# One run of 64x64 products in a fused attention and convolution step

## The reference

```python
q = einsum('bhwd,de->bhwe', x, Q_P)
k = einsum('bhwkd,de->bhwke', stk, K_P)      # stk: the 9 shifted views of x, zero-padded
v = einsum('bhwkd,de->bhwke', stk, V_P)
scores = einsum('bhwke,bhwe->bhwk', k, q) * mask
alpha = softmax(scores)
t = x + einsum('bhwk,bhwke->bhwe', alpha, v)
t_in = t
t = relu(conv(t, ff1_kernel) + ff1_bias)
t = relu(conv(t, ff2_kernel) + ff2_bias)
t = relu(conv(t, ff3_kernel) + ff3_bias)
return t_in + t
```

## Time and profile before

| | |
|---|---|
| median of 3 runs | 2117.69 us (2116.01 to 2118.15) |
| profiled execution | 2115.95 us, span 2114.2 us |
| TensorE busy | 2053.2 us, 97% |
| VectorE busy | 1856.8 us, 88% |
| ScalarE busy | 1068.6 us, 51% |
| weight loads busy | 1229.9 us, 58% |
| granted TensorE clock, mean | 0.992 |
| mean HBM and on-chip traffic of the DMAs | 152 GB/s |

### The profile page before, as it was taken

How to read it: one execution, slowest core, us unless ns; L and a number is a source line. 1 busy time by engine, 2 the same in 40 slices (tenths; PEclk the granted TensorE clock), 3 DMA queues, 4 the chain that set the end, 5 groups by cost and what they waited for, 6 DMA issues and landing times.

```text
span 2114.2 us, 61688 instructions
## 1 busy us (share of the span) xinstructions
PE 2053.2 (97%) x23866; PEld 1229.9 (58%) x23866; DVE 1856.8 (88%) x2756; ACT 1068.6 (51%) x3021; POOL 17.2 (1%) x28
## 2 busy tenths in 40 slices
PE   4899999999999999999999999999999999999997
PEld 3565555655565655655656655655656665665544
DVE  4698899899899899899889899899889899889885
ACT  3555555455455455455455455455455455455421
POOL 3000000000000000000000000000000000000000
PEclk9899999999999999999999999999999999999998
DMA  5555454454454454454455454454455454455432
GB/s 144 132 160 148 157 167 143 153 171 141 151 171 144 151 174 141 151 173 144 150 168 145 151 170 147 151 167 149 150 172 142 151 172 147 149 168 155 138 126 85
DMA packets 286054, 320.89 MB, mean 152 GB/s; under 512 B 87802, under 2 KB 220218, under 8 KB 279482
## 3 DMA queue, kind: packets, MB, share of 16 engines
q1 hardware_dynamic: 285982, 319.92, 50.0%
HBM read 150.23 MB, written 33.82 MB: 87 GB/s over the span
## 4 chain that ended last, share of the span: by engine, by line
PE 91%; DVE 5%; ACT 1%; issue 1%; DMA 1%; SPq 0%; DVEq 0%; ACTq 0%
PE conv_banks L496 31%; PE conv_banks L458 15%; PE conv_banks L521 13%; PE side_banks L521 13%; PE side_banks L439 5%; PE side_banks L418 4%; PE conv_banks L398 3%; PE side_banks L427 3%; PE side_banks L449 3%; PE side_banks L410 1%; DVE work L945 1%; ACT relued L766 1%; ACT prob L708 1%; DVE tf L852 0%; DVE negmax L831 0%
## 5 line engine op out<-in xcount | busy, mean ns | idle before, releaser
L496 PE MATMUL conv_banks<-dodd,w3f 128*64 128x512 f32 (+2 forms) x1616 | 492.9, 582 | 11.2 <-DVE work L912 9.5
L496 PE MATMUL conv_banks<-deven,w3f 128*64 128x512 f32 (+2 forms) x1616 | 496.7, 585 | 2.2 <-DVE prob L841 2.2
L708 ACT ACTIVATE prob<-side_banks,negmax 128x100 f32<-128x100 f32 x1024 | 341.7, 363 | 293.1 <-DVE negmax L831 293.1
L458 PE MATMUL conv_banks<-dt,w1f 128*64 128x256 f32 (+2 forms) x4128 | 395.5, 381 | 2.7 <-ACT rq L720 2.6
L458 PEld LDWEIGHTS conv_banks<-dt,w1f 128*64 128x64 f32 (+1 forms) x4128 | 224.3, 135 | 186.7 <-issue 99.5
L496 PEld LDWEIGHTS conv_banks<-dodd,w3f 128*64 128x64 f32 x1616 | 149.3, 138 | 246.3 <-issue 222.2
L945 DVE TENSOR_TENSOR work<-side_banks,work 128x1024 f32<-128x1024 f32 (+1 forms) x130 | 153.3, 1226 | 110.6 <-PE side_banks L521 110.6
L496 PEld LDWEIGHTS conv_banks<-deven,w3f 128*64 128x64 f32 x1616 | 147.8, 137 | 153.9 <-issue 114.2
L708 ACT ACTIVATION_READ_ACCUMULATOR prob<-side_banks,negmax 128x1 f32 x1024 | 230.3, 225 | 0.0
L720 ACT COPY rq<-conv_banks 128x512 f32<-128x512 f32 x128 | 74.0, 582 | 305.7 <-PE conv_banks L398 305.7
L725 ACT COPY probt<-side_banks 100x1024 f32<-100x1024 f32 x128 | 124.2, 1020 | 177.9 <-PE side_banks L427 177.9
(11 more groups left out here) (92 smaller groups left out, 3184.6 us busy)
## 6 DMA issues: line engine op xcount, KB each, us to landing
xk<-x_keys SPq DMA_DIRECT2D x65, 800.0 KB
xc<-x_bands SPq DMA_DIRECT2D x65, 650.0 KB, 4.9
xr<-x_bands SPq DMA_DIRECT2D x260, 128.0 KB, 2.9
dodd<-dodd SPq DMA_DIRECT2D x65, 512.0 KB, 3.0
out<-work SPq DMA_DIRECT2D x64, 512.0 KB, 2.7
xs<-x_bands SPq DMA_DIRECT2D x130, 128.0 KB, 3.1
dt<-dt SPq DMA_DIRECT2D x65, 256.0 KB, 4.9
deven<-deven SPq DMA_DIRECT2D x65, 256.0 KB, 3.1
```

The lines of the kernel that those rows point to most:

```text
L458: mm = nc.tensor.matmul(bank[(LOWER, UPPER)[o], n * 256 + lo * 64:n * 256 + hi * 64], w1f[i][rows, m, s, o * C:o * C + C], dt[rows, lo + s ...
L496: mm = nc.tensor.matmul(bank[rows, lo_ * 128:hi_ * 128], w3f[:, m, s, odd * C:odd * C + C], source[:, lo_ + s // 2:hi_ + s // 2, m], start ...
L708: last = nc.scalar.activation(prob[:, g, a], score_banks[g // 2][:, g % 2, a * KEYS:(a + 1) * KEYS], ACT.Exp, bias=negmax[:, g, a:a + 1], ...
```

## The change

The 64x64 products of an ordinary step stand in one run: v_product, masks and scores of half 0, outer quarters, masks and scores of half 1, and only then all the wholes. For this the halves of side_banks swap their roles (half 0 of the scores, mix and its turned weights in the far banks, half 1 and the value product in the near ones; streams 2 and 3 of ODD in the near banks, those of EVEN in the far ones), and waits are placed anew: v_product waits for outer ODD, masks of half 0 for outer EVEN. Wholes go image by image, and middle1 and keep_u2 are cut in two, one for each image. The turn of half 1 goes from ahead of conv2 into the second go_on2, with a wait of its own. On VectorE add_x goes ahead of the input transforms of ODD, and outer3 goes ahead of scalings 2 and 3 and the second u_low. On ScalarE both copies of r go ahead of the ReLUs.

```diff
-        score_banks = (near_banks, far_banks)
+        score_banks = (far_banks, near_banks)
...
-                for n, m in enumerate((0, 3) if outer else (2, 1)):
-                    for i in range(2):
+                for i in range(2):
+                    for n, m in enumerate((0, 3) if outer else (2, 1)):
...
-            def go_on2(G, k, j):
+            def go_on2(G, k, j, ahead=None):
 
                 pe.wait_ge(du_low, G * 2 + (j // 2 + 1))
                 for s in range(2):
+                    if ahead and s == 1:
+                        ahead()
...
-            def await_turn(b):
-                pe.wait_ge(y_ready, b * 2 + 4)
-                pe.wait_ge(prob_ready, b * GROUPS + 3 * GROUPS)
+            def await_turn(b, half):
+                if half == 0:
+                    pe.wait_ge(y_ready, b * 2 + 4)
+                pe.wait_ge(prob_ready, b * GROUPS + (2 * GROUPS + 2 + 2 * half))
...
                     quarters(k, False, True)
-                    wholes(k, False, False, lambda: await_v(G, b, att))
                     if att:
+                        pe.wait_ge(dve_read, outer_read(G, ODD, 1))
+                        pe.wait_ge(y_ready, b * 2 + 2)
+                        pe.sem_inc(phase_begun)
                         v_product(b)
+                    if att == ASK:
+                        pe.wait_ge(dve_read, outer_read(G, EVEN, 1))
+                        pe.wait_ge(r_ready, b * 2 + 5)
+                        pe.sem_inc(phase_begun)
+                        masks(0)
+                        scores(b + 2, 0)
+                        pe.wait_ge(r_ready, b * 2 + 6)
+                        pe.sem_inc(phase_begun)
                     quarters(k, True, True)
                     if att == ASK:
-                        masks(0)
-                        scores(b + 2, 0)
                         pe.wait_ge(t_ready, b * 2 + 2)
                         pe.sem_inc(phase_begun)
                         masks(1)
                         scores(b + 2, 1)
+                    wholes(k, False, False)
                     wholes(k, True, False)
...
-                conv3_tile(G, k, 3, (lambda: await_turn(b)) if att == ASK else None)
+                conv3_tile(G, k, 3, (lambda: await_turn(b, 0)) if att == ASK else None)
                 if att == ASK:
                     turn(b + 2, 0)
-                    turn(b + 2, 1)
                 begin2(G, k, 0, b, att)
                 go_on2(G, k, 0)
                 begin2(G, k, 1, b, att)
-                go_on2(G, k, 1)
+                go_on2(G, k, 1, (lambda: await_turn(b, 1)) if att == ASK else None)
+                if att == ASK:
+                    turn(b + 2, 1)
...
                 if att == ASK:
                     keep_r(b + 2, 0)
+                    keep_r(b + 2, 1)
                 if p is not None:
                     relu_conv2(G, None, ODD, 1)
-                if att == ASK:
-                    keep_r(b + 2, 1)
-                if p is not None:
                     relu_conv2(G, None, EVEN, 1)
-                keep_u2(G, k)
+                keep_u2(G, k, 0)
+                keep_u2(G, k, 1)
...
                     outer(G, None, ODD, 1)
                     outer(G, None, EVEN, 1)
-                    inputs(G, None, ODD, 0, 1)
-                    inputs(G, None, ODD, 1, 1)
                 if att:
                     add_x(k, b, par, 1)
                     add_x(k, b, par, 0)
                 if p is not None:
+                    inputs(G, None, ODD, 0, 1)
+                    inputs(G, None, ODD, 1, 1)
                     inputs(G, None, EVEN, 0, 1)
-                middle1(G, k)
+                middle1(G, k, 0)
+                middle1(G, k, 1)
...
                 u_low(G, k, 0)
+                outer3(G, k)
                 if att == ASK:
                     scale(b + 2, 2)
                     scale(b + 2, 3)
                 u_low(G, k, 1)
-                outer3(G, k)
                 finish(G, k, b)
```

More of the change, by code:

```diff
@@ L44 @@
 FILLS = 12
[L45 removed]
+ACT_READS, DVE_READS, RELUS = 5, 9, 3
 def fill_of(which, j):
@@ L148, in build @@
         r_banks = conv_banks[:, 2:4]
-        score_banks = (near_banks, far_banks)
+        score_banks = (far_banks, near_banks)
         def conv2_bank(which, j):
-            return (conv_banks if j < 2 else side_banks)[:, bank_of(which, j % 2)]
+            return conv_banks[:, bank_of(which, j)] if j < 2 else side_banks[:, 2 * (which == EVEN) + j % 2]
         const_in = sem("const_in")
@@ L223, in filled, with act_reads, middle_read, half1_done @@
             return G * FILLS + (fill_of(which, j) + 1)
[L225 to L230, removed]
+        def act_reads(G, which, behind=0, image=1):
+            n = {CONV1: 1 + image, CONV3: 3, ODD: 4, EVEN: 5}[which]
+            return G * ACT_READS + (n + ACT_READS - ACT_READS * behind - (2 if G is FINAL else 0))
+        def middle_read(G, which, behind=0, image=1):
+            n = {CONV1: 1 + image, CONV3: 4, ODD: 6, EVEN: 7}[which]
+            return G * DVE_READS + (n + DVE_READS - DVE_READS * behind - (3 if G is FINAL else 0))
         def outer_read(G, which, behind=0):
-            n = {CONV1: 2, CONV3: 4, ODD: 7, EVEN: 8}[which]
-            return G * DVE_READS + (n + DVE_READS - DVE_READS * behind - (2 if G is FINAL else 0))
+            n = {CONV1: 3, CONV3: 5, ODD: 8, EVEN: 9}[which]
+            return G * DVE_READS + (n + DVE_READS - DVE_READS * behind - (3 if G is FINAL else 0))
+        def half1_done(G, k, image):
+            return G * 8 + (4 if k == DRAIN else 2 * image + 2)
         def relus(G, which, behind=0):
@@ L438, in mix @@
                     for i, image in enumerate((LOWER, UPPER)):
-                        last = nc.tensor.matmul(near_banks[image, half, a * C:(a + 1) * C], xk[:, patch, image],
+                        last = nc.tensor.matmul(far_banks[image, half, a * C:(a + 1) * C], xk[:, patch, image],
                                                 probt[:, half, i if a < GROUP else 1 - i, a], start=True, stop=True)
@@ L481, in conv3_tile @@
                 if j == 0:
-                    pe.wait_ge(dve_read, middle_read(RUN, EVEN) if G is FINAL else middle_read(G, CONV1))
+                    pe.wait_ge(dve_read, middle_read(RUN, EVEN) if G is FINAL else middle_read(G, CONV1, image=0))
+                elif j == 1 and G is not FINAL:
+                    pe.wait_ge(dve_read, middle_read(G, CONV1))
                 elif j == 2 and G is not FINAL:
@@ L726, in keep_turned, with keep_u2 @@
                                score_banks[half][0:KEYS].rearrange("n i (a q) -> n i a q", q=C)).then_inc(probt_ready, 1)
[L728 removed]
+            def keep_u2(G, k, i):
                 lo, hi = pairs1(k)
[L730 to L734 removed]
+                act.wait_ge(conv1_done, half1_done(G, k, i))
+                if i == 0:
+                    act.wait_ge(dve_read, middle_read(G, ODD, 1))
+                nc.scalar.copy(m2_sb[:, 0, lo:hi, i],
+                               conv_banks[:, i, lo * 64:hi * 64].rearrange("c (s w) -> c s w",
+                                                                           w=WT)).then_inc(act_read, 1)
             def keep_m2(G, k, which):
@@ L940, in outer @@
                 lo, hi = pairs(which, k)
-                m03 = side_banks[:, which == EVEN::2, lo * 128:hi * 128]
+                m03 = side_banks[:, 2 * (which == EVEN):2 * (which == EVEN) + 2, lo * 128:hi * 128]
                 both = sums[which][:, lo:hi].rearrange("c s i (w n) -> c n (s i w)", n=2)
```

32 lines of the change are left out of this document (13 added, 19 removed).

## The result

| | before | after |
|---|---|---|
| median | 2116.85 us (2113.26 to 2118.15, 4 runs) | 2155.81 us (2155.41 to 2156.80, 4 runs) |
| profiled execution | 2115.95 us, span 2114.2 us | 2155.51 us, span 2153.7 us |
| ordinary step | 31.45 us | 32.24 us in the step shown, 32.21 in the median |

The account below looks back on a forecast made before the run. TensorE bounds the kernel before, VectorE about 2.7 us behind; after the change VectorE's tail decides. 57 attention steps at 0.45 and four k = 0 steps at 0.85 add 29 us: 2145 profiled, 2146 median, range 2122 to 2166.

Parts of the forecast that it names:

- The bound passes to VectorE: outer3 waits 1.9 us for conv3's last tile with scalings queued behind; TensorE's last conv2 pair then waits for middle EVEN.
- The step: Ordinary step, r_product to r_product: middle EVEN ends at 31.20, plus 0.70, gives 31.90 us, 0.45 longer.
- the tail: VectorE from outer3's start at 21.50 to middle EVEN's end at 31.20: 9.70 us of work.
- the border: From the end of VectorE's middle EVEN to the next r_product: at least 0.48, up to 0.85, taken as 0.70 us.
- the front: TensorE from r_product to conv3: 8.92 us plus 0.03 for tight waits, so 8.95 against 9.64.
- VectorE starts 0.13 behind that: add_x on VectorE begins 0.13 us after v_product ends at 2.88, a latency taken from outer ODD; add_x at 3.01.
- rival 3: Waits that fit by hundredths don't fit, each costing 0.15 us, all through the tail: step 32.3, 2170 us; 9%.
- The front's 0.72: Running 64x64 products together shortens TensorE's r_product to conv3 from 9.64 to 8.92 us, through fewer changes of tile shape.
- Rival 4: Running the products together removes no drain, the 0.20 and 0.24 us having another cause: step 32.2, 2163 us; 5%.
- two more waits: Behind await_next's wait for middle EVEN, TensorE's sequencer has these and the 0.215 us branch; up to 0.85 to r_product.
- Steps with k = 0: VectorE's 0.73 us idle ahead of add_x grows by up to 2.41; each costs 0.45 to 2.9, taken as 0.85 us.
- Rival 1: TensorE stays the bound and the saved 0.6 us arrive, needing a tail under 8.9: step 30.85, 2085 us; 8%.

Follow-up runs that it names:

- first experiment: The changed kernel with outer3 on VectorE put back behind scalings 2 and 3 and the second u_low: 2105.17 us, ratio 0.9952.
- the second: The kernel before with outer3 ahead of scalings 2 and 3 and the second u_low, and the second turning inside conv2: 2175.49 us, ratio 1.0287.
- ninth experiment: The changed kernel, VectorE's order kept, waiting last for v_product in add_x, outer EVEN before masks of half 0, middle EVEN in await_next: 2135.96 us.
- fifth experiment: The changed kernel with outer3 put back, add_x waiting for v_product last and masks of half 0 for outer EVEN last: 2093.69 us, ratio 0.9901.
- seventh experiment: The fifth experiment's kernel with the inner wholes moved between outer quarters and masks of half 1, two shape changes more: 2092.88 us, ratio 0.9898.
- sixth experiment: The changed kernel with TensorE's loop written out for two steps, so only every second step ends in a branch: 2154.68 us, ratio 1.0192.
- eighth experiment: The changed kernel with await_next on TensorE waiting for VectorE's middle EVEN last: 2146.70 us, ratio 1.0147.

## Why the prediction was right, and where its terms were off

**The bound passes to VectorE: right, and shown.** The first experiment takes 0.92 us a step away by moving outer3 alone, the second puts 1.07 on the kernel before. The idle time ahead of outer3 is 2.00 us (forecast 1.9), there is none ahead of middle ODD, TensorE stands in end2 (0.77 us) for middle EVEN, and from outer3's start to middle EVEN's end pass 9.69 us (forecast 9.70, whose terms stand in rows 5). Scalings 2 and 3 (L854) lay ready behind outer3: the last exponential ends at 1054.13, VectorE idles from 1055.72 to 1057.72. The Trainium skill, page "TensorE: Matmul & The Clock Gate", section "Architectural detail: the array is 16× 32×32, not 1× 128×128", has ScalarE and VectorE keep strictly to their queue; the trace agrees, with these 2.00 us.

**The step: 31.90 forecast, 32.24 in the step shown.** Measured against the forecast's terms the missing 0.34 are, in order: r_product to conv3 9.21 instead of 8.95 (+0.26), conv3 to outer3 12.62 instead of 12.55 (+0.07), the tail (-0.01), the border 0.72 instead of 0.70 (+0.02). So one term was mis-sized, the front. The step that failed is "VectorE starts 0.13 behind that" for add_x. It took the latency from outer ODD, where one wait decides, while add_x has three in a row; it was 0.36. With v_product 0.04 longer add_x came at 3.28 instead of 3.01, 0.27 later than forecast, and masks of half 1 at 4.72 instead of 4.45. The trace of the kernel before had the latency already: in its steps with k = 0 VectorE stands idle for v_product, which ends at 578.54, and add_x begins at 578.88, 0.34 later.

```profile
577.50 1.04 PE L449 MATMUL side_banks<-y,v_sb 64*64 64x512 f32 x8
```

The masks of half 0 came at 2.80 instead of 2.73, as two waits stand in a row there too, but this cost next to nothing (ninth experiment). This is rival 3's mechanism, and nearly its step of 32.3: the waits that fit by hundredths didn't fit, and all of it came through the tail. With the waits turned (ninth experiment) middle EVEN ends at 31.29, where the forecast has 31.20; the step is 31.80 and the forecast's 31.90, but there the border is 0.51 instead of 0.70.

**The total: 2146 forecast, 2155.8 measured, closer than the step.** The forecast's sum with 0.77 in place of 0.45 would be 57 x 0.77 + 3.4 = 47 us, that is 2165, the upper end of its range. That it came out 9 us lower is luck: the four steps with k = 1, counted among the 57, lose nothing, and the start and the end give some time back (below).

**The front's 0.72 without waits: nearly right in sum, partly for another reason.** In the fifth experiment the stretch is 9.02 us against 8.92. The 0.10 stand at v_product (0.94 instead of 0.91), at masks of half 0 (0.89 instead of 0.86) and at the outer quarters (0.91 instead of 0.87), all next to waits that are left there. But two changes of shape are only 0.21 to 0.25 of the 0.72 (seventh experiment, which has as many changes as the kernel before and still takes 9.23, not 9.64). The prediction laid the whole 0.24 between the two runs of wholes (2.02 and 1.78) to changes of shape. Between the same changes they take 1.88 us in the seventh experiment; 0.14 was a wait in the middle of them, for ScalarE's second copy of r. The weight load in the kernel before:

```profile
1018.28 0.20 PEld L458 LDWEIGHTS conv_banks<-dt,w1f 128*64 128x64 f32 x4 [0.38 <-ACT rq L720]
```

The first masks' 1.09 held the wait for add_x at their end, a further 0.2. The quarters ahead of the wholes take 0.96 in the seventh experiment and 1.07 in the kernel before; these 0.11 were not followed. Rival 4's step of 32.2 is met, but not by its mechanism: the front's 0.26 over the forecast are mostly waits, as the fifth experiment has 9.02. It is right that part of the 0.20 and 0.24 us came from something else than changes of shape.

**The border: 0.70 forecast, 0.72 measured, by the wrong reason.** The branch was to explain it; the sixth experiment puts that at 0.06, the eighth shows 0.2 for the waits standing behind the late one. The other half of the reason as the prediction put it ("two more waits") was the true one. In the loop the sequencer works out these waits' numbers in registers (the two lines of await_r in the kernel after, which the sequencer goes through once middle EVEN is over: instruction, count, duration in ns):

```profile
L393 PEldq FUSED_REGOPS  x53: 51/51/51, 164.2 to 2034.9; - x53
L394 PEldq FUSED_REGOPS  x53: 37/37/37, 164.3 to 2035.0; - x53
```

They put the pair 0.19 us later than without them (0.24 against 0.05 outside the loop), 0.1 us for each. The arithmetic isn't needed for that price: outside the loop, where the numbers are constants, one wait more behind the late one costs 0.1 us as well (eighth experiment).

**Steps with k = 0**: 33.13 to 33.81, +0.68 (forecast +0.85), with 2.72 us of idle time ahead of add_x. The very first of the four is 0.13 shorter instead. Not foreseen: the steps with k = 1 (31.65 to 31.60) lose nothing, as their conv3 is shorter (it ends 21.26 us after r_product, 21.68 in the other steps) and their border is 0.49. **Sum**: 53 steps in the loop at 0.77 make 40.8 us, the steps with k = 0 add 1.9 and those with k = 1 take 0.3; the profiled executions differ by 39.6, so what lies before and behind these steps gives back some 2.8, which were not followed further.

Rival 1 (a tail under 8.9) didn't come, since the tail was what its rows said. The first and the fifth experiment show how near it was: with outer3 left where it was, the same front and the split turns give 2105 us, and 2094 with two waits turned.

## What to carry to other kernels

Moving an instruction that waits for a late result ahead of ready work, on an engine that takes its list in order, costs the whole idle time as soon as the other engine waits for that list's end; look for what stands behind it before moving it. Where an instruction waits for several things, wait for the one that comes last at the end of the row: three such turns were worth 20 us here without moving any work, two of them nearly all of it. Then look in the trace on which instruction that wait ended up, as outside the loop the built order was another than the written one. A saving on the busiest engine arrives only as far as the next wait for the second-busiest: check what is late next, stretch by stretch.

## What the runs showed of the hardware

A fulfilled semaphore wait standing behind the late one is not free: two of them cost VectorE 0.21 us ahead of add_x (idle 0.72 to 0.51), and two in TensorE's await_next 0.19 us (0.24 to 0.05 behind middle EVEN), some 0.1 each. All four come with register arithmetic; one with a constant cost TensorE 0.1 us too (0.05 to 0.14, steps outside the loop of the eighth experiment). A change of tile shape on TensorE between 64x64 and 128x64 cost 0.10 to 0.12 us (0.21 to 0.25 for two). The loop's branch, 215 ns in the sequencer, showed in 0.06 us of the border even where the sequencer stood still just ahead of it.
